# The last two attention batches' output projection taken from the attention loop into the token search's rounds, and their gate logits made from a product of weights

## The chip, the cores and the metric

The kernel runs on one core of one Trainium2 chip, as one program. The metric is the device time of one execution, in microseconds (us); the lower the better. The times given are of whole executions. "PE" is TensorE, "DVE" VectorE, "ACT" ScalarE, "POOL" GpSimd and "SP" SyncE, which here only issues DMAs.

## What is computed

The input is 16 batches of 256 tokens with 256 features. A first block (folding, style blend, a two-layer FFN) makes `x1`. Then comes attention with 16 heads of 64, and a layer of 8 experts, each of which takes the 512 tokens with the highest gate for it:

```
qkv = (h @ Wqkv.T).reshape(b, n, 3, H, HD)
...
attn = jax.nn.softmax(scores, axis=-1)
o = jnp.einsum('bhnm,bhmd->bhnd', attn, v)
o = o.transpose(0, 2, 1, 3).reshape(b, n, H * HD)
x = x + o @ Wout.T
tok = x.reshape(-1, d)
gate = jax.nn.softmax(tok @ Wgate.T, axis=-1)
vals, idx = jax.lax.top_k(gate.T, k_cap)
g = _ln(tok[idx_flat], mlp_g, mlp_b).reshape(k_cap, E, d)
...
tok = tok.at[idx_flat].add(y.reshape(-1, d))
```

The change turns on `x + o @ Wout.T` (called x2 in the kernel) and on `tok @ Wgate.T` (the logits). The logits of a batch can be had without its x2, as x1 Wgate' + o (Wout' Wgate').

## The kernel before

The program has four parts, each with its own instruction streams, and a barrier of all engines between them: the first block, attention, the token search, the experts. Every product whose inputs need full precision is made of three matmuls on a high and a low half of each input (`product`, L147; the halves' names end in `_h` and `_l`); a matmul on plain `ident`, `proj` or `wgate` is one float32 product, which shows as two rows in the trace.

**Attention** runs in steps t, and batch b = t has its scores and softmax in step t. A step has 8 pairs s of heads. For each pair PE does, in program order: 12 score matmuls (L1107), the 8 transposes of the pair before (L1119), perhaps a fill (a few transposes or small products into bank 0, `fill`), the next batches' qkv products (`chunk`), and the products with v (L1134). DVE takes the scores' minimum (L1493), ACT the exponentials (L1262), POOL multiplies by the reciprocal of the sum (L1392), ACT and DVE copy the transposed probabilities (`pT`). The scores of the next pair wait for the exponentials of this one, since both use the same two banks. The order is written out by hand in tables (`TR_FILLS`, `PROJ_PAIRS`, `values_at`).

The output projection of batch t-1 is two rows of tokens with 24 matmuls of 128x256 each, in pairs 2 and 3 of step t (`project`). x1 is loaded again and added, x2 is stored to `out`, its layer norm to `x2_rows`, and its transposes (`x2` fill, L1205, then copied to `proj`) and the product with `wgate` (`gates` fill, L1210) give the logits. The last step with scores is t = 15 ("closing"), and there are no `chunk`s left in it. In it batch 14's projection stands in pairs 2 and 3, and batch 15's own is made piece by piece behind its pairs (`project_last`, L1158). `finish` (t = 16) does what is left of batch 15: two pairs of values, the last pieces of its projection, x2, its norm and its logits.

**The token search** finds each expert's 512th largest gate, two bits at a time, in 15 rounds. In a round DVE counts with two tests (L1749) and ACT with one (Sign, L1660), PE adds the counts over partitions (L1677), and DVE picks the next trial value (L1760 to L1770). Between these PE runs `idle_products(6)` (L1591): products whose result nobody reads. Meanwhile SP loads weights of the first two experts (`split_*`, made in attention) and raw weights of the third. POOL has nothing to do. The experts then gather rows from `x2_rows` by indirect DMA.

## Time and profile before

| | |
|---|---|
| median of 3 executions | 1431.31 us (1430.86 to 1431.76) |
| profiled execution | 1430.09 us, of which the trace spans 1428.3 us |
| PE busy | 1370.0 us, 96% |
| ACT, DVE, POOL busy | 1035.7, 960.9, 912.5 us |
| scores of batch 0 begin | 364.0 us |
| pair 2 of step t = 15 begins | 1125.6 us |
| search begins (first DVE instruction) | 1166.2 us |
| experts begin | 1205.3 us |

A row of a timeline gives start and duration in us, engine, source line, operation, what is written and read, how often, and in square brackets how long the engine had been idle before it and for whom. A matmul row's end is modelled and lies behind the next row's start: rates are read from starts. `PEclk` is the granted share of the full TensorE clock of 2.4 GHz.

### The profile page before, as it was taken

What the parts mean: (1) busy time and instruction counts of PE and PEld (TensorE: products, weight loads), DVE (VectorE), ACT (ScalarE), POOL (GpSimd) and SP (SyncE); (2) the same over time, 40 slices, a digit from 0 to 9 for tenths busy, and PEclk for the clock granted to TensorE, in tenths of its full rate; (3) what the DMA queues carried; (4) which work ended last, traced back from release to release, by engine and by line L of the source; (5) the groups of instructions that cost most, each with busy time, mean ns of one, the idle gap of its engine ahead of it and who ended that gap; (6) DMA issues with size and microseconds to landing.
All of it is one profiled execution on the core that took longest, in us unless ns stands there. A gap on an engine that the chain in (4) does not pass through costs nothing. (4 is left out here: it accounts for less than half of the span.)

```text
span 1428.3 us, 30431 instructions
## 1 busy us (share of the span) xinstructions
PE 1370.0 (96%) x10795; PEld 1184.1 (83%) x10795; DVE 960.9 (67%) x2191; ACT 1035.7 (73%) x2703; POOL 912.5 (64%) x855
## 2 busy tenths in 40 slices
PE   7899999997999999999999999999999988999996
PEld 6799999996688887887888888788888678889896
DVE  6876677654776676676667667667756568678763
ACT  5566666565898889889889888988988732476662
POOL 2576666652678768867877876886777620354643
PEclk9899999999999999999999999999999999999999
DMA  5342222110100100110110010011011046145522
GB/s 159 122 122 67 68 68 69 50 51 23 38 9 31 53 23 31 53 45 9 53 46 31 31 53 28 26 53 45 9 45 46 31 143 258 45 104 155 138 34 30
DMA packets 61638, 89.04 MB, mean 62 GB/s; under 512 B 6144, under 2 KB 50992, under 8 KB 58800
## 3 DMA queue, kind: packets, MB, share of 16 engines
q1 hardware_dynamic: 53232, 75.82, 16.4%
q0 software_dynamic: 6144, 8.39, 3.6%
q10 hardware_dynamic: 2112, 2.88, 0.6%
q8 instruction: 87, 1.43, 0.4%
q14 instruction: 63, 0.52, 0.1%
HBM read 61.90 MB, written 25.18 MB: 61 GB/s over the span
## 5 line engine op out<-in xcount | busy, mean ns | idle before, releaser
L1392 POOL TENSOR_TENSOR prob<-prob,share_p 128x512 f32<-128x512 f32 x256 | 271.6, 1067 | 196.1 <-DVE share_p L1499 195.6
L1493 DVE TENSOR_REDUCE shift<-bank 128x2 f32<-128x512 f32 x256 | 164.7, 685 | 185.9 <-PE bank L1107 185.8
L1262 ACT ACTIVATE prob<-bank,shift 128x256 f32<-128x256 f32 x512 | 237.8, 479 | 63.9 <-DVE shift L1493 63.8
L147 PE MATMUL bank<-wqkv_h,rowsT_h 128*128 128x512 f32 x384 | 159.3, 415 | 2.0 <-PEq L311 1.7
L147 PE MATMUL bank<-wqkv_h,rowsT_l 128*128 128x512 f32 x384 | 151.7, 395 | 0.0
L147 PE MATMUL bank<-wqkv_l,rowsT_h 128*128 128x512 f32 x384 | 151.3, 394 | 0.0
L1119 PE MATMUL bank<-ident,prob 128*128 128x128 f32 x1024 | 143.0, 281 | 1.3 <-POOL prob L1392 1.3
L1380 POOL TENSOR_TENSOR landing<-landing,rq 128x512 f32<-128x512 f32 x128 | 131.1, 1046 | 10.1 <-DVE rq L1447 10.1
L1134 PE MATMUL bank<-pT,landing 128*64 128x256 f32 x1024 | 126.2, 386 | 1.7 <-ACT pT L1351 1.7
L1119 PEld LDWEIGHTS bank<-ident,prob 128*128 128x128 f32 x1024 | 109.6, 141 | 21.7 <-POOL prob L1392 4.2
L1262 ACT ACTIVATION_READ_ACCUMULATOR prob<-bank,shift 128x1 f32 x512 | 107.3, 210 | 0.0
L1286 ACT ACTIVATE landing<-bank,cols 128x512 f32<-128x512 f32 x128 | 101.9, 796 | 5.8 <-PE bank L1200 4.2
L644 POOL TENSOR_TENSOR hid_l<-hid,hid_h 128x512 fp32r<-128x512 f32 x64 | 86.3, 1358 | 30.6 <-ACT hid_h L540 29.9
L536 ACT ACTIVATE hid<-bank,cols 128x256 f32<-128x256 f32 x128 | 53.3, 470 | 68.1 <-PE bank L147 67.9
L1134 PEld LDWEIGHTS bank<-pT,landing 128*64 128x64 f32 x1024 | 67.3, 137 | 40.8 <-issue 9.2
L1107 PE MATMUL bank<-kT_h,qT_h 64*128 64x256 f32 x512 | 85.6, 330 | 3.1 <-ACT prob L1262 3.1
L1489 DVE TENSOR_REDUCE ssq<-raw_sq 128x8 f32<-128x512 f32 x128 | 85.8, 672 | 3.2 <-ACT raw_sq L1308 2.6
L1524 DVE COPY pT<-bank 128x512 f32<-128x512 f32 x128 | 87.1, 681 | 0.4 <-PE bank L1119 0.4
L1306 ACT ACTIVATE landing<-bank 128x512 f32<-128x512 f32 x128 | 80.0, 625 | 9.1 <-PE bank L147 9.0
L1200 PE MATMUL bank<-ident,landing 128*128 128x128 f32 x512 | 78.4, 276 | 8.2 <-ACT landing L1286 3.7
L147 PEld LDWEIGHTS bank<-wqkv_h,rowsT_h 128*128 128x128 f32 x384 | 73.2, 191 | 15.5 <-issue 2.4
L147 PEld LDWEIGHTS bank<-wqkv_h,rowsT_l 128*128 128x128 f32 x384 | 72.7, 189 | 15.7
(324 smaller groups left out, 4518.3 us busy)
## 6 DMA issues: line engine op xcount, KB each, us to landing
landing<-in_fc1s SPq DMA_DIRECT2D x6, 1024.0 KB, 4.9
landing<-in_fc2s SPq DMA_DIRECT2D x6, 1024.0 KB, 5.1
rows<-in_x SPq DMA_DIRECT2D x16, 256.0 KB, 2.9
xT<-in_xT SPq DMA_DIRECT2D x16, 256.0 KB, 2.7
x_again<-in_x SPq DMA_DIRECT2D x16, 256.0 KB, 2.8
x_rows<-x SPq DMA_DIRECT2D x16, 256.0 KB, 3.2
rows<-x_rows SPq DMA_DIRECT2D x16, 256.0 KB, 3.1
x<-x_rows SPq DMA_DIRECT2D x16, 256.0 KB, 2.9
```

The costliest lines, as they stand in the source:

```text
L147: last = nc.tensor.matmul(out, a, b, start=(n == 0), stop=(n == 3 * len(ks) - 1))
L644: nc.gpsimd.tensor_tensor(hid_l[:, 2 * g:2 * g + 2, :], hid[:, 2 * g:2 * g + 2, :], hid_h[:, 2 * g:2 * g + 2, :].bitcast(F32), ALU.subtrac ...
L1107: mm = nc.tensor.matmul(score_bank[side][:, n * T:(n + 1) * T], q[r, at, n * P:(n + 1) * P], k[r, at, :], start=(i == 0), stop=(i == 2))
L1119: last = nc.tensor.transpose(pT_bank[side][:, m * T + n * P:m * T + (n + 1) * P], prob[q % 2 * 2 + side][:, n, m * P:(m + 1) * P], ident[: ...
L1134: last = nc.tensor.matmul(values_bank(b, q)[side * HD:(side + 1) * HD, :], v[its][:, m, h * HD:(h + 1) * HD], pT[q % 2 * 2 + side][:, m, : ...
L1262: last = nc.scalar.activation(prob[at][:, n, :], score_bank[side][:, n * T:(n + 1) * T], ACT.Exp, bias=shift[:, at, n:n + 1], scale=-1.0, ...
L1286: nc.scalar.activation(raw_block(j), tr[:, :].rearrange("p (m n) -> p m n", m=4), ACT.Identity, bias=cols[:, g + 1:g + 2], scale=cols[:, g ...
L1380: nc.gpsimd.tensor_tensor(part, part, rq[:, n, c * 8:(c + 1) * 8].unsqueeze(2).to_broadcast([P, 8, HD]), ALU.mult).then_inc(normed, 1)
L1392: nc.gpsimd.tensor_tensor(prob[at][:, :, :], prob[at][:, :, :], share[:, at, :].unsqueeze(2).to_broadcast([P, TT, T]), ALU.mult).then_inc( ...
L1489: nc.vector.tensor_reduce(ssq[:, n, c * 8:(c + 1) * 8], raw_sq[c % 2][:, :].rearrange("p (h d) -> p h d", h=8), AX, ALU.add).then_inc(summ ...
L1493: nc.vector.tensor_reduce(shift[:, s % 2 * 2 + side, :], score_bank[side][:, :].rearrange("p (n m) -> p n m", n=TT), AX, ALU.min).then_inc ...
L1524: nc.vector.tensor_copy(pT[q % 2 * 2 + 1][:, :, :].rearrange("p m n -> p (m n)"), pT_bank[1][:, :]).then_inc(pT_dve, 1)
```

## The change

In words: `project_last` and the projections of batches 14 and 15 leave attention. `kept` holds the halves of the output projection's weights and of o in memory that outlives attention; batch 14's o is also stored to DRAM (`keep_o`, 8 DMAs of 256 KB) and read back in the search, while batch 15's stays in place. For the logits, batch 0's step makes `wc` = Wout' Wgate' on PE (`logit_weights`, after pair 0's chunks: 16 float32 products with 8 columns) from `woutT`, which SP loads into the four `pT` tiles; DVE splits it in pair 1. `logits_of` then multiplies `wc` (16 columns: high and low part of 8) with o, 16 matmuls a batch, and the `gates` fill adds two small products to bring them to the logits of x1, whose transposes now fill from the reloaded x1.

In the search PE does 32 `late_step`s of three 128x256 matmuls: four steps ahead of the rounds, three in each of rounds 0 and 1, two in each of rounds 2 to 12. Every eighth step (in rounds 1, 4, 8 and 12) also adds x1 by a product of `late_x` with `ident`. Fewer idle products stand behind them, so that one idle product goes for two matmuls; the six before the gates' transposes and the six behind them go too. ACT takes the rows out of the banks and does the layer norm within the rounds, with small steps on POOL. SP stores x2 and its norm at the end of the search. The second expert's first weights (2 MB) are loaded after the first gathers, since batch 14's o uses their tile. The raw piece of expert weights now lands in `ew_l`, so its next load waits for the store of the one before.

```
+LATE = 2
+LATE_FROM = NB - LATE
+O_STORED, LATE_STORED, WC_IN = 16 * 7, 32, 80
+LATE_ORDER = [NB - 1] + list(range(LATE_FROM, NB - 1))
...
+CLOSING_FILLS = {(NB - 1, 9): (NB - 2, "x2"), (NB - 1, 11): (NB - 2, "gates"), (NB - 1, 13): (NB - 1, "x2"), (NB, 3): (NB - 1, "gates")}
+LATE_PAIR = {False: PROJ_PAIRS[0], True: PROJ_PAIRS[1]}
...
+                def keep_o(b, qs):
+                    for q in qs:
+                        wait(sp, o_lo, PAIRS, b, q + 2)
+                        for n, part in enumerate((o_h, o_l)):
+                            sp.dma_start(o_kept[b - LATE_FROM][n][:, q * T:(q + 2) * T],
+                                         o_part(part, q, b % 2, 2).bitcast(F32)).then_inc(o_stored, 16)
+
                 def step(t, odd):
+                    if t == -1:
+                        for q in range(4):
+                            sp.dma_start(pT[q][:, :, :], a["woutT"][:, q * T:(q + 1) * T].rearrange("(k p) n -> p k n", p=P)).then_inc(wc_in, 16)
...
                         load_piece(0, 0)
+                    if is_late(t - 1) and live(t):
+                        keep_o(t - 1, (0, 2, 4, 6))
...
+                        sp.wait_ge(ew_stored, 32 * (t + 1))
                         load_piece(t + 1, 1 - odd)
...
+                def logit_weights():
+                    pe.wait_ge(wc_in, WC_IN + 64)
+                    for m in range(PAIRS):
+                        for k in range(KT):
+                            last = nc.tensor.matmul(o_bank[:, m * E:(m + 1) * E], pT[m // 2][:, k, m % 2 * P:(m % 2 + 1) * P], wgate[:, k, :],
+                                                    start=(k == 0), stop=(k == KT - 1))
+                    last.then_inc(wc_made, 1)
...
-                def project_last(k, its):
...
+                def logits_of(b, half, its):
+                    wait(pe, o_lo, PAIRS, b, 4 * half + 4)
+                    if half == 0:
+                        if live(b + 2):
+                            wait(pe, chunk_out, 12, b + 2, 7)
+                        else:
+                            wait(pe, chunk_out, 12, NB - 1, 12)
+                            wait(pe, out_proj, TT, b - 1, TT)
+                    for k in range(4 * half, 4 * half + 4):
+                        for n, part in enumerate((o_h, o_l)):
+                            last = nc.tensor.matmul(chunk_bank[0][0:2 * E, 0:T], wc[:, k, :], part[:, o_at(k, its), :],
+                                                    start=(k == 0 and n == 0), stop=(k == PAIRS - 1 and n == 1))
+                    if half == 1:
+                        last.then_inc(tr_proj, TT)
...
-                                last = nc.tensor.matmul(fill_bank(b)[:, n * E:(n + 1) * E], x2T[:, k, n * P:(n + 1) * P], wgate[:, k, :],
-                                                        start=(k == 0), stop=(k == KT - 1))
+                                last = nc.tensor.matmul(tr[:, n * E:(n + 1) * E], x2T[:, k, n * P:(n + 1) * P], wgate[:, k, :],
+                                                        start=(k == 0), stop=(k == KT - 1 and not is_late(b)))
+                            if is_late(b):
+                                last = nc.tensor.matmul(tr[:, n * E:(n + 1) * E], from_o[:, n * P:(n + 1) * P], parts_of[:, :], start=False, stop=True)
                         last.then_inc(tr_gates, 1)
...
                 def finish(t, its):
-                    fill(t, 1)
                     values(t - 1, PAIRS - 2, its)
                     transposes(t - 1, PAIRS - 1)
-                    project_last(PAIRS - 3, its)
+                    logits_of(t - 1, 0, its)
+                    values(t - 1, PAIRS - 1, its)
+                    logits_of(t - 1, 1, its)
                     fill(t, 3)
-                    values(t - 1, PAIRS - 1, its)
-                    project_last(PAIRS - 2, its)
-                    project_last(PAIRS - 1, its)
...
+                        if first(t) and s == 0:
+                            logit_weights()
+                        if first(t) and s == 2:
+                            pe.wait_ge(wc_done, NB + 2)
                         if not closing(t):
-                            if s in PROJ_PAIRS and live(t - 1):
+                            if s in PROJ_PAIRS and live(t - 1) and not is_late(t - 1):
                                 project(t - 1, PROJ_PAIRS.index(s), 1 - odd)
+                            if s == LATE_PAIR[False] and live(t - 1) and is_late(t - 1):
+                                logits_of(t - 1, 0, 1 - odd)
+                                logits_of(t - 1, 1, 1 - odd)
...
-                        if closing(t) and s in PROJ_PAIRS:
-                            project(t - 1, PROJ_PAIRS.index(s), 1 - odd)
-                        if closing(t) and s >= 4:
-                            for k in range(0 if s == 4 else s - 3, s - 2):
-                                project_last(k, odd)
                         if closing(t):
+                            if s == LATE_PAIR[True]:
+                                logits_of(t - 1, 0, 1 - odd)
+                                logits_of(t - 1, 1, 1 - odd)
...
+                def logits_out(b):
+                    wait(act, tr_proj, TT, b, TT)
+                    wait(act, tr_gates, 1, b - 1, 1)
+                    nc.scalar.activation(from_o[:, :], chunk_bank[0][0:2 * E, 0:T], ACT.Copy).then_inc(out_proj, TT)
...
+LATE_FIRST, LATE_STEPS = 4, [3] * 2 + [2] * 11 + [0] * 2
+TAKEN_IN, SPREAD_IN, NORMED_IN = {2: 0, 5: 1, 10: 2, 13: 3}, {3: 0, 7: 1, 11: 2, 14: 3}, {6: 0, 9: 1, 13: 2}
...
+                    load_late_x(0)
...
+                    for i in range(1, LATE):
+                        load_late_x(i)
+                        load_late_o(i)
+                    load_halves(sp, w1_in, (w1_h, w1_l), halves[0:2], 0)
                     for e in range(EARLY):
-                        load_halves(sp, w1_in, (w1_h, w1_l), halves[0:2], e)
                         load_halves(sp, w2_in, (w2_h, w2_l), halves[2:4], e)
+
                     load_raw(sp, w1_raw, a["fc1s"], EARLY, 0, 0)
                     load_raw(sp, w2_raw, a["fc2s"], EARLY, 0, 1)
                     sp.dma_start(b1[:, :], a["b1s"]).then_inc(b1_in, 16)
                     sp.dma_start(b2[:, :, :], a["b2s"].unsqueeze(0).to_broadcast([P, E, D])).then_inc(b2_in, 16)
+                    for i, b in enumerate(LATE_ORDER):
+                        sp.wait_ge(late_normed, NB + TT * (i + 1))
+                        for rows, tile, last in ((x2_rows, late_n[i], last_rows), (out, late_x[i], last_out)):
+                            sp.dma_start(rows[bass.ds(b * T, T), :].rearrange("(t p) d -> p t d", p=P),
+                                         tile[:, :, :]).then_inc(last if i == LATE - 1 else late_stored, 16)
+                    sp.wait_ge(late_stored, LATE_STORED + 32 * (LATE - 1))
...
+                    def take(i):
+                        act.wait_ge(late_made, NB + i + 1)
+                        nc.scalar.activation(row(late_x, i), late_bank(i), ACT.Copy, accum_out=late_sum[:, i:i + 1]).then_inc(late_taken, 1)
+
+                    def spread_of(i):
+                        act.wait_ge(late_taken, NB + i + 1)
+                        nc.scalar.activation(late_mean[:, i:i + 1], late_sum[:, i:i + 1], ACT.Copy, scale=-1.0 / D).then_inc(late_centred, 1)
+                        act.wait_ge(late_centred, NB + i + 1)
+                        nc.scalar.activation(late_dead[:, :], row(late_x, i), ACT.Square, bias=late_mean[:, i:i + 1],
+                                             accum_out=late_sq[:, i:i + 1]).then_inc(late_squared, 1)
+
+                    def norm(i):
+                        act.wait_ge(late_rooted, NB + i + 1)
+                        nc.scalar.activation(row(late_n, i), row(late_x, i), ACT.Identity, bias=late_shift[:, i:i + 1],
+                                             scale=late_root[:, i:i + 1]).then_inc(late_normed, 1)
...
+                        if n in TAKEN_IN:
+                            take(TAKEN_IN[n])
+                        if n in SPREAD_IN:
+                            spread_of(SPREAD_IN[n])
+                        if n in NORMED_IN:
+                            norm(NORMED_IN[n])
+                    norm(LATE * TT - 1)
...
-                    idle_products(6)
...
+                    def late_step(i, k):
+                        j, rows = i // TT, slice(i % TT * P, (i % TT + 1) * P)
+                        high, low = late_o[j]
+                        if k == 0 and i % TT == 0 and j > 0:
+                            pe.wait_ge(late_in[j], 16 + 48)
+                        if k == HW // P - 1 and i == 0:
+                            pe.wait_ge(late_in[0], 16 + 16)
+                        if k == 0 and i >= 2:
+                            pe.wait_ge(late_taken, NB + i - 1)
+                        for m, (o, w) in enumerate(((high, wo_h), (high, wo_l), (low, wo_h))):
+                            nc.tensor.matmul(late_bank(i), o[:, k, rows], w[:, k, :], start=(k == 0 and m == 0), stop=False)
+                        if k == HW // P - 1:
+                            nc.tensor.matmul(late_bank(i), ident[:, :], late_x[j][:, i % TT, :], start=False, stop=True).then_inc(late_made, 1)
+
+                    for k in range(LATE_FIRST):
+                        late_step(0, k)
+                    done = LATE_FIRST
...
-                        idle_products(6)
+                        for _ in range(LATE_STEPS[n]):
+                            late_step(done // (HW // P), done % (HW // P))
+                            done += 1
+                        idle_products(6 - LATE_STEPS[n] * 3 // 2, 2, 384)
...
+                    if t == -3:
+                        for half in gathered:
+                            sp.wait_ge(half, 32)
+                        load_halves(sp, w1_in, (w1_h, w1_l), halves[0:2], 1)
...
+                        if first(later):
+                            pool.wait_ge(last_rows, 16 * (LATE_FROM + 1))
```

PE in step t = 15's end and `finish`, before: the last rows ahead of the search. The six L1158 rows are the last piece of batch 15's projection.

```order
L1158 MATMUL bank<-wout_h,o_h 128x256
L1158 MATMUL bank<-wout_l,o_h 128x256
L1158 MATMUL bank<-wout_h,o_l 128x256
L1158 MATMUL bank<-wout_h,o_h 128x256
L1158 MATMUL bank<-wout_l,o_h 128x256
L1158 MATMUL bank<-wout_h,o_l 128x256
L1205 MATMUL bank<-ident,x 128x128 x4
L1210 MATMUL bank<-wgate,proj 128x8 x4
```

The same place in the changed kernel (L1157 transposes, L1172 values, L1194 `logits_of`, L1249 and L1252 the `gates` fill).

```order
L1157 MATMUL bank<-ident,prob 128x128 x8
L1194 MATMUL bank<-kept,wc 16x256 x8
L1172 MATMUL bank<-pT,landing 64x256 x4
L1194 MATMUL bank<-kept,wc 16x256 x8
L1249 MATMUL bank<-wgate,proj 128x8 x2
L1252 MATMUL bank<-parts_of,from_o 128x8
L1249 MATMUL bank<-wgate,proj 128x8 x2
L1252 MATMUL bank<-parts_of,from_o 128x8
```

The transposes of x stand two pairs earlier, and the projection's pieces between transposes and values are gone.

PE at the start of the search in the changed kernel, rounds 0 and 1; before, six L1591 products stood first, six behind the gates' transposes, and six in every round.

```order
L1813 MATMUL bank<-kept 128x256 x12
L1822 MATMUL bank<-ident,gates 128x128 x2
L1827 MATMUL bank<-base,same 128x4
L1830 MATMUL bank<-count,same 128x4
L1832 MATMUL bank<-base,same 128x4
L1813 MATMUL bank<-kept 128x256 x9
L1662 MATMUL bank<-ident 128x128 x2
L1830 MATMUL bank<-count,same 128x4
L1832 MATMUL bank<-base,same 128x4
L1813 MATMUL bank<-kept 128x256 x3
L1815 MATMUL bank<-late_x,ident 128x256
L1813 MATMUL bank<-kept 128x256 x6
```

The late matmuls stand between one round's total and the next one's, where the idle ones stood.

PE in step t = 0 of the changed kernel, from pair 0's last chunk to pair 1's scores (L1145, before L1107).

```order
L147 MATMUL bank<-wqkv_h,rowsT_h 128x512
L147 MATMUL bank<-wqkv_l,rowsT_h 128x512
L147 MATMUL bank<-wqkv_h,rowsT_l 128x512
L1130 MATMUL bank<-wgate,pT 128x8 x16
L1145 MATMUL bank<-kT_h,qT_h 128x256 x2
```

The L1130 row is new; before, the scores followed the chunk.

## Rows read from the trace of the kernel before

**Rows 1.** The page: busy time, and PE's granted clock in 40 slices.

```profile
PE 1370.0 (96%) x10795; PEld 1184.1 (83%) x10795; DVE 960.9 (67%) x2191; ACT 1035.7 (73%) x2703; POOL 912.5 (64%) x855
...
PEclk9899999999999999999999999999999999999999
```

**Rows 2.** Timeline of PE, t = 15: the first score row of pairs 2 to 7.

```profile
1125.58 0.38 PE L1107 MATMUL bank<-kT_h,qT_h 64*128 64x256 f32 x2
...
1131.60 0.39 PE L1107 MATMUL bank<-kT_h,qT_h 64*128 64x256 f32 x2
...
1137.60 0.38 PE L1107 MATMUL bank<-kT_h,qT_h 64*128 64x256 f32 x2
...
1142.17 0.39 PE L1107 MATMUL bank<-kT_h,qT_h 64*128 64x256 f32 x2
...
1146.01 0.39 PE L1107 MATMUL bank<-kT_h,qT_h 64*128 64x256 f32 x2
...
1149.85 0.39 PE L1107 MATMUL bank<-kT_h,qT_h 64*128 64x256 f32 x2
```

**Rows 3.** Timeline of PE, pair 2: first and last of 24 projection matmuls; pair 1's gates.

```profile
1124.60 1.06 PE L1210 MATMUL bank<-wgate,proj 128*128 128x8 f32 x8
...
1128.53 0.39 PE L147 MATMUL bank<-wout_h,o_h 128*128 128x256 f32 x1
...
1131.39 0.28 PE L147 MATMUL bank<-wout_h,o_l 128*128 128x256 f32 x1
```

**Rows 4.** Timeline, `finish` and the change to the search.

```profile
1156.32 0.69 DVE L1524 COPY pT<-bank 128x512 f32<-128x512 f32 x1 [0.17 <-PE bank L1119]
...
1158.08 1.08 PE L1134 MATMUL bank<-pT,landing 128*64 128x256 f32 x8
...
1159.62 0.42 DVE L1512 TENSOR_TENSOR o_l<-bank,o_h 128x256 fp32r<-128x256 f32 x1 [1.96 <-ACT o_h L1334]
...
1161.75 0.75 DVE L1517 TENSOR_TENSOR x<-bank,x 128x256 f32<-128x256 f32 x2 [1.70 <-DMA x<-x_rows]
...
1165.06 0.18 ACT L1293 ACTIVATE logit<-bank 128x16 f32<-128x16 f32 x1 [1.21 <-PE bank L1210]
...
1166.19 0.18 DVE L1704 MEMSET units<- 128x1 f32 x5 [0.87 <-PEq L1052]
```

**Rows 5.** Timeline, t = 0 (pairs 0 to 4): PE at the new products' place, and its waits.

```profile
367.86 0.39 PE L1107 MATMUL bank<-kT_h,qT_h 64*128 64x256 f32 x2
...
375.45 0.66 PE L1200 MATMUL bank<-ident,landing 128*128 128x128 f32 x4 [0.34 <-POOL landing L1380]
...
382.36 0.39 PE L1107 MATMUL bank<-kT_h,qT_h 64*128 64x256 f32 x2 [1.38 <-ACT prob L1262]
...
384.77 1.11 PE L1119 MATMUL bank<-ident,prob 128*128 128x128 f32 x4 [0.84 <-POOL prob L1392]
```

**Rows 6.** Timeline, a round of the search.

```profile
1176.52 0.51 ACT L1660 ACTIVATE signs<-key,trial 128x256 bf16<-128x256 f32 x1 [1.30 <-DVE trial L1770]
...
1177.33 0.08 DVE L1749 DVE_READ_ACCUMULATOR count_junk<-key,trial 128x1 fp32r x1
...
1177.47 0.27 PE L1677 MATMUL bank<-count,same 128*128 128x4 f32 x1
...
1177.71 1.58 PE L1591 MATMUL bank<-ident 128*128 128x128 f32 x12
```

**Rows 7.** Timeline of PE, first block: float32 products with 256 columns.

```profile
10.54 2.07 PE L388 MATMUL bank<-landing 16*128 16x256 f32 x4
```

**Rows 8.** Windows (stretch, length, each engine's busy time, PEclk, DMA share, GB/s).

```profile
380.00:384.00 4.00, 2.55 (x26) 1.97 (x23) 3.93 (x11) 3.60 (x11) 2.41 (x3) 1.00 0.00 0
384.00:387.00 3.00, 2.23 (x10) 2.14 (x11) 1.87 (x4) 1.25 (x5) 3.00 (x4) 0.53 0.78 252
1162.00:1166.00 4.00, 1.69 (x12) 1.39 (x12) 2.41 (x9) 0.78 (x2) 0.69 (x1) 0.98 0.19 66
1166.00:1169.00 3.00, 2.85 (x12) 2.63 (x12) 2.23 (x17) 0.42 (x1) 0.00 (x0) 0.50 0.70 184
```

232 lines of the change are left out of this document (138 added, 94 removed).

## The prediction

> **What bounds the kernel now.** I read the page first: PE is busy 96% of the span and its clock is granted nearly everywhere [rows 1]. So each added product costs its time wherever PE has no gap, and each removed one pays only where nothing else takes its place. The page can't say which of the two holds at the four places that the change touches; the timelines do.
>
> In step t = 15 the pairs take 6.02, 6.00, 4.57, 3.84 and 3.84 us (pairs 2 to 6, from the starts of their scores [rows 2]). The last two are the floor that no removal gets under: a pair's scores, DVE's minimum, four exponentials on ACT, and the next scores wait for them. The same floor shows in t = 0, where PE has nothing else to do and waits 1.38 us for ACT [rows 5]. Pairs 2 to 4 lie above it because of the projection.
>
> In the search a round takes 1.90 us, and it is DVE's chain that sets it: DVE's second count ends at 1177.41 and the total starts at 1177.47. The idle products are 12 rows from 1177.71 on that end 1.58 us later by a modelled end [rows 6]. I take 0.12 us a row, so they keep PE 12 x 0.12 = 1.44 us, and with the two small products ahead of them (0.24) PE needs 1.68 of the 1.90. Its slack is 0.22 us a round. ACT is idle 1.30 us before each Sign [rows 6].
>
> **The pairs of t = 15.** A projection of 128 tokens is 24 matmuls; their first and last starts are 2.86 us apart [rows 3], 0.12 us each, and the pair spends 3.07 us on them (1128.53 to 1131.60 [rows 2, 3]). Pair 2 loses one and falls to the floor: 6.02 to 3.85, -2.2. Pair 3 loses 24 and gets `logits_of(14)`, 16 matmuls that also stream 256 columns, 2.0 us: 6.00 to 4.95, -1.05; it stays above the floor. Pair 4 loses 12 (1.5 us) and gets four transposes: 4.57 to 3.85, -0.7. Pair 5 gets the `gates` fill. Before, pair 1's fill took 1124.60 to 1125.58 [rows 2, 3], 0.98 us for 8 rows; the two new products add 4 rows, 0.45. PE's work in a pair without extras is 2.95 us (1125.58 to 1128.53 [rows 2, 3]), so 2.95 + 0.98 + 0.45 = 4.4 against 3.84: +0.55. Pair 6 stays. Sum -3.4; I keep 0.6 either way, for the loss of the x2 work on DVE and POOL and for how well the copies of ACT fit in.
>
> **`finish` and the way to the search.** Pair 7's values can start once DVE's copy ends at 1157.01 [rows 4]; they started at 1158.08 because the gates of batch 14 and a piece of the projection stood ahead. Now only 8 matmuls (1.0 us) stand there, so about 1157.2: -0.87. The low half of o then ends at 1159.17 instead of 1160.04 [rows 4]. Before, from there: six matmuls, a wait for x1's DMA until 1161.75, two adds, transposes, copy, gates, logit at 1165.06 to 1165.24. Now: 8 matmuls (1.2 with the tail), ACT's copy of 16 rows (0.4), 12 gate rows (1.5), the logit (0.25): 1159.17 + 3.4 = 1162.6. The search's first DVE instruction came at 1166.19, 0.95 after the logit; batch 15's norm and its store are gone too, so I take 0.8: 1163.4. That is -2.8, between -2.2 and -3.2.
>
> **Step t = 0.** 16 float32 products are 32 rows. The nearest rows have the same weights' size and the same 8 columns: 8 in 0.98 us [rows 2, 3]. 32 cost 3.8 us, right before pair 1's scores, which started at 367.86 behind the chunk without a wait [rows 5]. Nothing covers it. What may give some back are the waits for POOL (0.34 and 0.84 [rows 5]) since POOL gets ahead while PE is held; the 1.38 is the floor and stays. Bounds +2.6 and +3.9; I put +3.8 in the sum and the return, 0.8, beside the clock below. The woutT load (1 MB at the start of attention) and DVE's split are over long before they are needed.
>
> The Trainium skill, "TensorE: Matmul & The Clock Gate", part 1, says that the distance of two matmuls' starts never drops below about 25 ns however small they are. By that floor 32 rows would cost 0.8 us and the sum below would be 3.0 lower. The row (0.12 us at 8 columns) disagrees by a factor of five here, as each of these products loads 128 new columns of weights; I go by the row.
>
> **The rounds.** Four steps ahead of the rounds run while PE would have idled. In the rounds three matmuls at 0.12 replace one and a half products of two rows: 6 matmuls + 6 rows is again 12. Round 0 has 13 units, within the slack. But rounds 1, 4, 8 and 12 add a float32 product of 256 columns. Four rows of 256 columns took 2.07 us at half clock [rows 7], so a product's two rows take 0.5 at full clock. Rounds 4, 8, 12: 0.24 + 1.44 + 0.5 + 0.1 for the change of kind = 2.28, +0.38 each; round 1: 2.5, +0.6. Sum +1.8, between 0 (if the matmuls pack tighter than the idle rows) and 3.3 (0.1 more in each of 15 rounds). ACT's new work in a round is one or two operations on 256 columns like Sign's 0.51 [rows 6], with a small one beside; it fits into the 1.30 idle, tightest in rounds 13 and 14, and POOL is free.
>
> **Loads and stores.** SP loads as much in the search as before but for 0.5 MB. The last rows' norm follows the last Sign by a square, three small POOL steps and itself; DVE still has the ranks to work out then, and the first gather needs indices that are only made in the experts' part. In attention the piece's later load waits for two stores, a pair or so, and is not read before pair 2 of the next step. All of this I put at 0; if that cover is gone, a late store holds the first gather, microsecond for microsecond.
>
> **Sum.** -3.4 - 2.8 + 3.8 + 1.8 = -0.6 us against the profiled execution's 1430.09.
>
> **The clock.** It is granted at 0.53 in 384 to 387 behind a stretch in which PE waited for ACT and POOL and was busy 2.55 of 4 us, and at 0.50 in 1166 to 1169 behind one with 1.69 of 4 us busy, among it 8 gate rows of 8 columns [rows 8]. A row pair that runs at 1.2 instead of 2.4 GHz takes double. The 3.8 us of narrow rows in t = 0 look more like the second of these stretches than like any full one, and dense chunks follow. If the clock falls there for as long as the 3 us of either low row, PE does half the work in them and loses about 1.7 with the edges. With the 0.8 that POOL's lead gives back I add 0.9: together +0.3. The median of the plain runs is 1.2 above the profiled one; I carry the difference over: 1431.3 + 0.3 = **1431.6 us**.
>
> **Rivals.**
> 1. *The terms nearly cancel* (as above), 1429 to 1434: chance 0.50.
> 2. *The clock falls and costs twice.* In t = 0 it is low during part of the narrow rows and during the chunks behind them (two low stretches, +3.4). At the search's start the six products behind the gates' transposes are gone, so PE stands still some 2 us right after a low stretch; if the clock is low in the first rounds, 13 rows take 3.1 us and a round costs 1.2 to 1.5 more. -0.6 + 3.4 + 1.5 = +4.3: 1435.6. It decides for slower from +2.9 on, which means a second low stretch. For it: rows 8. Against: most of the search's stretch is dense. Chance 0.25. The Trainium skill, same page, part 1, states that the throttled clock is the default and activity releases it; rows 8 agree with it in both places.
> 3. *The rows are cheap.* The narrow products cost near the page's floor, or PE's slack and POOL's lead swallow them, and the closing rounds fit: -0.6 - 3.0 = -3.6, 1427.7. For it: the idle rows' true need is not measured, only bounded. Against: 0.98 us for 8 narrow rows, 16 times in the trace. Chance 0.20.
> 4. *The last rows' store is late* and the first gather waits: each microsecond beyond its cover costs one, so 2 to 5 late gives 1433 to 1437. Against: by then nothing else is queued on SP. Chance 0.05.
>
> **Numbers.** About 0.2% (2.9 us) is what a measurement of this kernel can tell from no change. Faster by more: rival 3 and the low end of 1, 0.23. Slower: 2, 4 and the high end of 1, 0.27. Same: 0.50. Range: the lower bounds of the terms give -4.0 - 3.2 + 2.6 + 0.5 = -4.1, 1427.2; the upper end lies 0.9 above rival 2, for a round more at the low clock: 1436.5.
>
> **What would show each step.** In the changed profile: pairs 2 to 5 of t = 15 at 3.9, 4.95, 3.9, 4.4; the search's first MEMSET about 6.2 us less behind pair 2 than before; 32 narrow rows of 0.12 us in t = 0 and PEclk behind them; rounds 1, 4, 8, 12 at 2.3 to 2.5 and the others at 1.90; from the search's start to the experts 40.9 instead of 39.1. I'm wrong if other rounds grow too, if the narrow rows run at another rate, or if the first gather waits for the store.

## The result, and the profile after

The changed kernel takes 1435.06 us (median of 11 executions, 1429.36 to 1436.26), the kernel before 1431.32 us (11 executions on the same chip, 1428.83 to 1433.11). The ratio is 1.0024, with a 95% interval of 1.0015 to 1.0033: 3.7 us slower, more than the 0.2% that can be told from no change. The profiled execution of the changed kernel took 1433.18 us with a span of 1431.4, 3.1 more than the one before. Four executions among those of the experiments below took 1688 to 2651 us instead of about 1430; their ratios leave these out, their medians don't.

Taking the same points of both traces gives the balance (shift is after minus before, in us):

| point | before | after | shift | what this part added |
|---|---|---|---|---|
| scores of pair 1, t = 0 | 367.86 | 372.45 | +4.59 | +4.59 |
| scores of pair 2, t = 0 | 373.00 | 379.63 | +6.63 | +2.04 |
| scores of pair 0, t = 1 | 410.22 | 416.50 | +6.28 | -0.35 |
| scores of pair 2, t = 15 | 1125.58 | 1132.63 | +7.05 | +0.77 |
| scores of pair 7, t = 15 | 1149.85 | 1154.15 | +4.30 | -2.75 |
| first DVE instruction of the search | 1166.19 | 1168.22 | +2.03 | -2.27 |
| experts' first idle products | 1205.30 | 1209.77 | +4.47 | +2.44 |
| first fc1 of the experts | 1224.11 | 1227.39 | +3.28 | -1.19 |

PE's timeline of the changed kernel at t = 0, from pair 0's last chunk on. It answers to the score rows in [rows 5]:

```profile
364.02 0.39 PE L1145 MATMUL bank<-kT_h,qT_h 64*128 64x256 f32 x2
...
367.56 0.40 PE L147 MATMUL bank<-wqkv_h,rowsT_l 128*128 128x512 f32 x1
367.79 4.73 PE L1130 MATMUL bank<-wgate,pT 128*128 128x8 f32 x32
372.45 0.58 PE L1145 MATMUL bank<-kT_h,qT_h 64*128 64x256 f32 x2
...
374.03 1.97 PE L1157 MATMUL bank<-ident,prob 128*128 128x128 f32 x8
...
379.63 0.39 PE L1145 MATMUL bank<-kT_h,qT_h 64*128 64x256 f32 x2
...
388.66 0.39 PE L1145 MATMUL bank<-kT_h,qT_h 64*128 64x256 f32 x2 [1.37 <-ACT prob L1306]
391.07 1.11 PE L1157 MATMUL bank<-ident,prob 128*128 128x128 f32 x4 [0.85 <-POOL prob L1448]
```

The 32 narrow rows hold PE for 372.45 - 367.79 = 4.66 us. About 20 of them start before 370, 0.11 us each; the last 12 take 0.2 each. Pair 1 behind them takes 7.18 us (372.45 to 379.63) where it took 5.14, without a wait of its own: its eight transposes last 1.97 us, at full clock such a group lasts 1.09. Pair 2 takes 5.22 us instead of 5.55, since the wait of 0.34 for POOL [rows 5] is gone. The last two rows show that the waits for ACT and POOL further on are as long as before (1.37 and 0.85; 1.38 and 0.84 in [rows 5]), so POOL's lead gave back 0.3 and no more. The windows of the same stretch (PEclk, the granted clock, is the third number from the end):

```profile
core 0: us, PE busy (x) PEld busy (x) DVE busy (x) ACT busy (x) POOL busy (x), PEclk, DMA share, GB/s
364.00:370.00 6.00, 6.00 (x46) 5.34 (x45) 4.45 (x9) 5.87 (x18) 2.04 (x2) 1.00 0.00 0
370.00:374.00 4.00, 4.00 (x25) 3.78 (x24) 0.00 (x0) 0.02 (x1) 0.00 (x0) 0.51 0.00 0
374.00:377.00 3.00, 3.00 (x15) 2.95 (x14) 2.38 (x5) 1.13 (x5) 0.84 (x1) 0.51 0.00 0
377.00:380.00 3.00, 3.00 (x18) 2.25 (x18) 2.25 (x9) 3.00 (x9) 1.10 (x2) 1.00 0.35 93
```

PE counts as fully busy in all four, and yet it runs at 1.2 GHz from about 370 to 377. Neither PE's busy share nor that of its weight loads (PEld, 3.78 of 4 us from 370 on) tells such a stretch; the clock column does.

One trace could be chance, but there are four with these rows in t = 0 (the changed kernel, e4_search, e4_again and e9_behind below), and in each the clock is low from 370 or 371 to 377 or 378. In the ten others, that of the kernel before among them, it is 1.00 from 366 to 380.

PE's timeline from `finish` to round 1 of the search. It answers to [rows 4] and [rows 6]; L1194 are the logits' matmuls on wc, L1813 the late matmuls, L1815 a closer, L1662 the idle products:

```profile
1161.33 1.08 PE L1172 MATMUL bank<-pT,landing 128*64 128x256 f32 x8
1163.36 1.11 PE L1194 MATMUL bank<-kept,wc 128*16 128x256 f32 x8 [0.94 <-DVE kept L1575]
1165.02 0.64 PE L1249 MATMUL bank<-wgate,proj 128*128 128x8 f32 x4 [0.56 <-issue]
1165.59 0.59 PE L1252 MATMUL bank<-parts_of,from_o 16*128 16x8 f32 x2
1166.11 1.02 PE L1249 MATMUL bank<-wgate,proj 128*128 128x8 f32 x4
...
1168.19 2.90 PE L1813 MATMUL bank<-kept 128*128 128x256 f32 x12 [0.53 <-PEq L1064]
1171.27 0.69 PE L1822 MATMUL bank<-ident,gates 128*128 128x128 f32 x2 [0.18 <-DVE gates L1875]
1173.93 0.27 PE L1827 MATMUL bank<-base,same 128*128 128x4 f32 x1 [1.98 <-DVE same L1909]
...
1175.95 0.37 PE L1830 MATMUL bank<-count,same 128*128 128x4 f32 x1
1176.18 0.35 PE L1832 MATMUL bank<-base,same 128*128 128x4 f32 x1
1176.39 0.99 PE L1813 MATMUL bank<-kept 128*128 128x256 f32 x3
1177.18 1.05 PE L1815 MATMUL bank<-late_x,ident 128*128 128x256 f32 x2
1177.67 1.69 PE L1813 MATMUL bank<-kept 128*128 128x256 f32 x6
1179.20 0.61 PE L1662 MATMUL bank<-ident 128*128 128x128 f32 x4
1179.57 0.25 PE L1830 MATMUL bank<-count,same 128*128 128x4 f32 x1
```

PE stands still for 1.98 us where twelve idle rows stood, and round 1 takes 1179.57 - 1175.95 = 3.62 us instead of 1.90. Windows of the changed kernel over the same place:

```profile
1168.00:1172.00 4.00, 3.59 (x14) 2.92 (x14) 2.62 (x20) 0.42 (x1) 0.00 (x0) 0.50 0.47 142
1172.00:1176.00 4.00, 2.07 (x17) 2.07 (x17) 3.37 (x17) 1.20 (x4) 0.00 (x0) 0.93 1.00 349
1176.00:1179.00 3.00, 3.00 (x14) 2.82 (x14) 2.01 (x10) 1.08 (x4) 0.00 (x0) 0.50 1.00 421
```

Low, then nearly full while PE is busy 2.07 of 4 us, then low again during round 1. Rounds 4, 8 and 12 (each with a closer) take 2.05 to 2.07 us, rounds without one 1.88 to 1.93, but for round 6, which takes 2.42 as it did before. Round 4's closer and what stands behind it, at full clock:

```profile
1184.39 0.59 PE L1815 MATMUL bank<-late_x,ident 128*128 128x256 f32 x2
1184.82 0.83 PE L1662 MATMUL bank<-ident 128*128 128x128 f32 x6
1185.40 0.25 PE L1830 MATMUL bank<-count,same 128*128 128x4 f32 x1
```

### The profile page after: what moved, and what is told of

It is laid out like the page before. It is cut to its first block and busy times, and to the rows that moved or that the text cites. A ratio compares the mean times of both kernels' runs of the same rounds, so it can differ in the third digit from the quotient of the medians.

```text
span 1431.4 us, 30415 instructions
## 1 busy us (share of the span) xinstructions
PE 1370.6 (96%) x10769; PEld 1182.9 (83%) x10769; DVE 956.8 (67%) x2178; ACT 1042.8 (73%) x2727; POOL 912.8 (64%) x864
## 5 line engine op out<-in xcount | busy, mean ns | idle before, releaser
L147 PE MATMUL bank<-kept 128*128 128x256 f32 x1440 | 183.1, 285 | 0.0
L147 PEld LDWEIGHTS bank<-kept 128*128 128x128 f32 x1440 | 175.3, 191 | 0.0
L1157 PE MATMUL bank<-ident,prob 128*128 128x128 f32 x1024 | 144.5, 282 | 1.9 <-POOL prob L1448 1.9
L1157 PEld LDWEIGHTS bank<-ident,prob 128*128 128x128 f32 x1024 | 110.6, 142 | 23.1 <-POOL prob L1448 5.3
L1172 PE MATMUL bank<-pT,landing 128*64 128x256 f32 x1024 | 126.2, 386 | 3.1 <-ACT pT L1409 3.1
L656 POOL TENSOR_TENSOR kept<-hid,kept 128x512 fp32r<-128x512 f32 x64 | 86.3, 1357 | 31.0 <-ACT kept L552 30.4
L1172 PEld LDWEIGHTS bank<-pT,landing 128*64 128x64 f32 x1024 | 67.3, 136 | 42.8 <-issue 9.4
L147 PE MATMUL bank<-kept,w_h 128*128 128x256 f32 x512 | 95.8, 287 | 0.0
L147 PE MATMUL bank<-ew_h,kept 128*128 128x256 f32 x512 | 94.1, 282 | 0.0
L1145 PE MATMUL bank<-kT_h,qT_h 64*128 64x256 f32 x512 | 85.8, 331 | 4.0 <-ACT prob L1306 3.8
```

What stands on the lines that cost most here:

```text
L147: last = nc.tensor.matmul(out, a, b, start=(n == 0), stop=(n == 3 * len(ks) - 1))
L656: nc.gpsimd.tensor_tensor(hid_l[:, 2 * g:2 * g + 2, :], hid[:, 2 * g:2 * g + 2, :], hid_h[:, 2 * g:2 * g + 2, :].bitcast(F32), ALU.subtrac ...
L1145: mm = nc.tensor.matmul(score_bank[side][:, n * T:(n + 1) * T], q[r, at, n * P:(n + 1) * P], k[r, at, :], start=(i == 0), stop=(i == 2))
L1157: last = nc.tensor.transpose(pT_bank[side][:, m * T + n * P:m * T + (n + 1) * P], prob[q % 2 * 2 + side][:, n, m * P:(m + 1) * P], ident[: ...
L1172: last = nc.tensor.matmul(values_bank(b, q)[side * HD:(side + 1) * HD, :], v[its][:, m, h * HD:(h + 1) * HD], pT[q % 2 * 2 + side][:, m, : ...
```

## Experiments

Each was timed in five rounds beside the kernel before. Since the kernel before read 1431.32, 1431.98, 1430.72 and 1430.88 us in the four sets of runs, the ratios to it compare better than the medians. Experiments 1 to 4 ran in one set, 5 to 8 in the next, the last four in a third, each set on another chip.

| run | median us | ratio to before, 95% |
|---|---|---|
| changed kernel | 1435.06 | 1.0024 (1.0015 to 1.0033) |
| e1_dense | 1433.40 | 1.0009 (1.0001 to 1.0018) |
| e2_none | 1429.54 | 0.9985 (0.9976 to 0.9994) |
| e3_early | 1429.77 | 0.9988 (0.9979 to 0.9996) |
| e4_search | 1439.18 | 1.0051 (1.0038 to 1.0063) |
| e5_finish | 1429.94 | 0.9994 (0.9985 to 1.0003) |
| e6_open | 1428.18 | 0.9982 (0.9973 to 0.9991) |
| e7_both | 1428.95 | 0.9990 (0.9981 to 0.9999) |
| e8_close | 1427.50 | 0.9980 (0.9971 to 0.9989) |
| e9_behind | 1437.58 | 1.0047 (1.0034 to 1.0060) |
| e4_again | 1437.49 | 1.0048 (1.0035 to 1.0061) |
| e10_early_e4 | 1428.61 | 0.9987 (0.9977 to 0.9996) |
| e11_early_all | 1427.75 | 0.9978 (0.9970 to 0.9987) |

**e1_dense**: the narrow products against dense ones of as many rows.

```
-                    for m in range(PAIRS):
-                        for k in range(KT):
-                            last = nc.tensor.matmul(o_bank[:, m * E:(m + 1) * E], pT[m // 2][:, k, m % 2 * P:(m % 2 + 1) * P], wgate[:, k, :],
-                                                    start=(k == 0), stop=(k == KT - 1))
+                    last = nc.tensor.matmul(o_bank[:, 0:PAIRS * E], pT[0][:, 0, 0:P], wgate[:, :, :].rearrange("p k e -> p (k e)")[:, 0:1].to_broadcast([P, PAIRS * E]),
+                                            start=True, stop=True)
                     last.then_inc(wc_made, 1)
+                    for _ in range(15):
+                        nc.tensor.matmul(o_bank[:, 384:512], ident[:, :], ident[:, :], start=True, stop=True)
```

> Changed kernel with the 16 products of 8 columns in t = 0 (32 narrow rows) replaced by one product of 64 columns and 15 idle products of 128 x 128 on ident: as many float32 rows, but dense ones. The product of wout and the router's weights is left out, so wc holds other numbers. Theory A (the narrow rows let the clock fall, and the pair behind them pays double): the rows still cost about 3.9 us, but pair 1 behind them takes 5.1 us again instead of 7.2, PEclk stays at 1.00 from 368 to 380; 1432.7, that is 2.4 below the changed kernel. Theory B (only the time of the rows counts, and the clock falls in t = 0 for another reason, or its fall only moves): a low stretch stays within 368 to 380 and the time stays within 0.5 of the changed kernel's, 1435.

It came out 0.15% (2.1 us) below the changed kernel, theory A's side; each of the two ratios is good to 0.09%, so the time alone would be thin. The trace decides it. Its timeline and windows at t = 0:

```profile
366.07 0.39 PE L1145 MATMUL bank<-kT_h,qT_h 64*128 64x256 f32 x2
...
369.83 0.33 PE L1128 MATMUL bank<-wgate,pT 128*128 128x64 f32 x2
370.00 3.57 PE L1132 MATMUL bank<-ident 128*128 128x128 f32 x30
373.50 0.39 PE L1145 MATMUL bank<-kT_h,qT_h 64*128 64x256 f32 x2
...
378.64 0.39 PE L1145 MATMUL bank<-kT_h,qT_h 64*128 64x256 f32 x2
```

```profile
370.00:374.00 4.00, 4.00 (x40) 3.88 (x41) 1.15 (x2) 2.04 (x6) 1.15 (x2) 1.00 0.00 0
374.00:377.00 3.00, 3.00 (x27) 2.64 (x25) 2.01 (x5) 1.77 (x6) 0.47 (x1) 1.00 0.00 1
377.00:380.00 3.00, 3.00 (x24) 2.30 (x23) 2.93 (x11) 3.00 (x10) 1.87 (x3) 1.00 0.28 87
```

30 rows of 128 columns and two of 64 take 3.67 us, and pair 1 behind them 5.14, all at 1.00. So the rows with sixteen times the columns came out cheaper: at full clock a row costs about the same (0.12 and 0.11 us), and behind these the clock stayed. The dense rows differ from the narrow ones in more than width: they read one tile, `ident`, which is mostly zeros, again and again. The experiment shows that it isn't the number of rows; width and contents it doesn't tell apart.

**e2_none** takes the narrow products out, but for one.

```
-                    for m in range(PAIRS):
-                        for k in range(KT):
...
+                    last = nc.tensor.matmul(o_bank[:, 0:PAIRS * E], pT[0][:, 0, 0:P], wgate[:, :, :].rearrange("p k e -> p (k e)")[:, 0:1].to_broadcast([P, PAIRS * E]),
+                                            start=True, stop=True)
```

> Changed kernel with the 16 products of 8 columns in t = 0 replaced by a single one of 64 columns: the product of wout and the router's weights is left out, so wc holds other numbers. Theory A (rows 3.8 to 4.6, and their low clock 2): t = 0 costs nothing more than before, 6.3 below the changed kernel, 1428.8, below the kernel before by 2.5. Theory B (what t = 0 lost comes back by itself as later waits shrink or grow): 3.8 or less is won, 1431.3 or more.

0.39% (5.6 us) below the changed kernel: theory A. With e1_dense this splits the price of t = 0: 0.24% (3.5 us) for the rows' time, 0.15% (2.1 us) for what they do to the clock. The traces give 3.4 and 3.0, by the way from pair 0's scores to pair 2's (15.61 us in the changed kernel, 12.57 in e1_dense, 9.17 in e2_none). That the whole gained less has a place in the traces too: rounds 0 and 1 of the search both run at the low clock in e1_dense and e2_none (6.99 and 6.97 us together), while the changed kernel's trace has 5.64.

**e3_early** puts them into gaps of step t = -1.

```
+WEIGHTS_AT = {5: (0, 1), 7: (1, 4), 8: (4, 6), 10: (6, 7), 12: (7, 8)}
-                        if first(t) and s == 0:
-                            logit_weights()
+                        if t == -1:
+                            logit_weights(2 * s)
                         fill(t, 2 * s)
...
+                            if t == -1:
+                                logit_weights(2 * s + 1)
                             fill(t, 2 * s + 1)
```

> Changed kernel with the same 16 products of 8 columns spread over half-pairs 5, 7, 8, 10 and 12 of step t = -1, ahead of idle fills in which PE waits 0.6 to 2.0 us each for something else; nothing is left out. Theory A (these gaps are free): all of the 6.3 us of t = 0 goes, or 5.5 if two of the gaps are too short; 1429. Theory B (the gaps are there since PE is ahead of a chain that its fills belong to, so that a product put in them pushes the chain, or the clock falls there instead): half of it or more stays, 1431 to 1433.

0.36% (5.2 us) below the changed kernel and 0.12% below the kernel before: theory A. The scores of pairs 0 to 3 of t = 0 start at 364.01, 367.87, 372.99 and 378.55, within 0.01 us of the kernel before: the gaps were free. Not all that its trace gains over the kernel before is the change's doing: step t = 0 takes 44.82 us against 46.21, since the low stretch of 384 to 387 [rows 8] isn't there. But its search opens worse than the changed kernel's:

```profile
1155.00:1158.00 3.00, 1.76 (x14) 1.34 (x14) 0.42 (x1) 0.54 (x2) 0.00 (x0) 1.00 0.00 0
1158.00:1162.00 4.00, 3.47 (x18) 3.36 (x19) 1.53 (x15) 0.60 (x2) 0.00 (x0) 0.57 0.22 49
1162.00:1166.00 4.00, 1.84 (x8) 1.14 (x7) 2.92 (x14) 0.60 (x2) 0.00 (x0) 0.50 0.82 257
1166.00:1170.00 4.00, 4.00 (x20) 4.00 (x20) 2.27 (x12) 0.60 (x2) 0.00 (x0) 0.50 1.01 420
1170.00:1172.00 2.00, 2.00 (x9) 1.82 (x9) 1.28 (x7) 1.07 (x4) 0.00 (x0) 0.50 0.97 406
```

One unbroken low stretch from the finish on; rounds 0 and 1 take 3.44 and 3.60 us.

**e4_search** changes the search and leaves t = 0 as it is.

```
                     last.then_inc(tr_gates, 1)
+                    idle_products(6, 2, 384)
                     for n in range(DIGITS):
...
-                        idle_products(6 - LATE_STEPS[n] * 3 // 2, 2, 384)
+                        idle_products(6 - LATE_STEPS[n] * 3 // 2 - (2 if n in (1, 4, 8, 12) else 0), 2, 384)
```

> Changed kernel with six idle products back behind the gates' transposes at the search's start, and two idle products fewer in each of rounds 1, 4, 8 and 12, where a closing product of 256 columns is added; nothing is left out. Theory A (the stand-still of PE at the start makes the second low stretch, and round 1 takes 3.6 us for it): round 1 is 1.9 again, rounds 4, 8 and 12 1.9 instead of 2.05; 2.1 below the changed kernel, 1433.0. Theory B (the clock falls there anyway, owing to the way that the finish goes): only the closing rounds give back, 0.45; 1434.6, with a low stretch still between 1172 and 1180.

Neither theory: 0.27% (3.9 us) above the changed kernel. In its profiled execution (1434.33 us, the fastest of six) the rounds are as meant, 1.90 in rounds 1, 4, 8 and 12. The other five took 1437.05 to 1439.88 with a mean granted clock of 0.977 to 0.982 against 0.983 in the profiled one. By the mean clock, that is more time at 1.2 GHz; no trace shows where.

**e5_finish, e6_open, e7_both** fill gaps of e3_early with idle products: e5_finish by the `idle` lines in `finish` (and a wait for ACT's last exponentials ahead of them, since they write to a scores' bank), e6_open by the two `idle_products(6, 2, 384)`, e7_both by all.

```
                 def finish(t, its):
+                    wait(pe, exped, H, t - 1, H)
+                    idle(4)
                     values(t - 1, PAIRS - 2, its)
...
+                    idle(3)
                     logits_of(t - 1, 1, its)
+                    idle(2)
                     fill(t, 3)
...
                     done = LATE_FIRST
+                    idle_products(6, 2, 384)
                     pe.wait_ge(gated, 1)
...
                     last.then_inc(tr_gates, 1)
+                    idle_products(6, 2, 384)
```

> The kernel with the early narrow products (e3_early, 1429.8) with nine idle products more in the finish, in gaps in which PE waits: four ahead of the values of pair 6 (a gap of 1.13 us), three ahead of the second half of the logits (0.94), two ahead of the gates (0.56); nothing is left out. Theory A (it is PE's standing still in the finish that starts the 13.7 us low stretch from 1158 on): the stretch is gone or shorter, rounds 0 and 1 take 1.9 us each again instead of 3.4 and 3.6; 1426.7, 3.1 below e3_early. Theory B (the stand-still behind the finish, at the search's start, does it): the low stretch only starts later and still covers both rounds; 1429.5 to 1430.5.

> e3_early with twelve idle products more at the search's start: six behind the four late steps, where PE waits for the gates, and six behind the gates' transposes, where it waits for the first counts (1.98 us); nothing is left out. Theory A (those two gaps keep the low stretch going once it has begun): it ends earlier, round 1 at least is 1.9 again; 1428.0, 1.8 below e3_early. Theory B (at half clock the idle products take 2.9 us for six and push the gates' transposes and the first base product): 1431 to 1434. The run in which six of these products and fewer in the closing rounds gave 1439.2 speaks for B.

> e3_early with the idle products of both e5_finish and e6_open; nothing is left out. If the finish alone starts the low stretch, the twelve at the start are free at full clock: 1426.7 as e5_finish. If only both gaps together keep the clock: 1426.5, with e5_finish and e6_open at 1429 or above. If the clock falls whatever PE does there: 1431 to 1434.

e5_finish is not below e3_early (0.9994 against 0.9988; the intervals overlap). Its windows:

```profile
1160.00:1165.00 5.00, 4.35 (x34) 3.96 (x32) 1.21 (x14) 0.73 (x3) 0.00 (x0) 1.00 0.07 8
1165.00:1168.00 3.00, 0.62 (x4) 0.20 (x2) 2.20 (x9) 0.32 (x2) 0.00 (x0) 1.00 0.64 195
1168.00:1172.00 4.00, 2.99 (x14) 2.99 (x15) 2.88 (x15) 1.13 (x4) 0.00 (x0) 0.57 1.03 389
```

The finish and the late steps now run at full clock, but in the next stretch PE is busy 0.62 of 3 us and the clock falls behind it, over rounds 0 and 1 as before (3.44 and 3.53). That is theory B: a low stretch comes later and the time stays. e6_open and e7_both brought rounds 0 and 1 back to 2.01 and 2.19, and 2.01 and 2.18. e6_open's ratio is 0.06% below e3_early's, not the 0.12% of theory A, and the intervals overlap. The price named in its theory B is also paid: from pair 7's scores to the first base product it takes 1168.54 - 1147.42 = 21.1 us instead of 1165.67 - 1146.48 = 19.2, since twelve idle rows at half clock stand ahead of the gates' transposes. Idle products in the finish added nothing to that: e7_both's 0.9990 is no better than e3_early's 0.9988, and none of the three times expected of it (1426.5, 1426.7, 1431 or more) came.

**e8_close** is e3_early with the second edit of e4_search.

> e3_early with two idle products fewer in each of rounds 1, 4, 8 and 12, nothing else; nothing is left out. It undoes one half of what e4_search did. Theory A (rounds 4, 8 and 12 are 0.15 longer for PE's work alone): 0.45 to 0.6 below e3_early, 1429.2. Theory B (this half cost e4_search its 4 us, by low stretches within the search): 1433, with a low stretch behind one of these rounds.

0.9980: theory B's 1433 is out. Rounds 4, 8 and 12 take 1.90 again, as theory A has it, and round 1 3.14 instead of 3.60; together 0.9 us in the trace, and 0.08% (1.1 us) was measured, with intervals that overlap e3_early's. e4_search's loss isn't this half's.

**e9_behind, e4_again, e10_early_e4, e11_early_all** follow that loss and look for the best version. e9_behind is the first edit of e4_search alone, e10_early_e4 both edits on e3_early, e11_early_all the edits of e6_open and e8_close together.

> The changed kernel with one half of e4_search alone: the six idle products behind the gates' transposes; nothing is left out. Theory A (e4_search's 1439.2 belongs to these products): 1438 or more. Theory B (it belongs to the pair of edits, or to that set of runs and not to the code): 1433.5, 1.5 below the changed kernel, from round 1 at 1.9 instead of 3.6.

> e4_search once more, unchanged, beside e9_behind on one chip. If its 4 us over the changed kernel are the code's, 1438 to 1440 again, and its low stretches in the slower runs tell where; if they were that set's, 1433, as its profile alone would have it (1434.3 with rounds 1, 4, 8 and 12 at 1.90).

> e4_search's two edits on e3_early, where nothing is left of the narrow products in t = 0; nothing is left out. From the traces so far: the way from pair 7 to the first base product and rounds 0 and 1 take 23.9 in e4_search, 26.2 in e3_early, 25.9 in e8_close; rounds 4, 8 and 12 give 0.45. Theory A (the pieces add): 1427.0, 2.7 below e3_early. Theory B (e4_search's edits cost wherever they stand): 1433 or more.

> e6_open (1428.2) and e8_close (1427.5) together: e3_early with twelve idle products at the search's start and two fewer in each closing round; nothing is left out. If the two gains add (e6_open's 0.06% and e8_close's 0.08% below e3_early): 1427.0. If fewer idle products in round 1 undo what the twelve hold (round 1 was 2.18 in e6_open): round 1 at half clock and 1428 or more.

e4_again repeats e4_search, and e9_behind gives the same loss by the six products behind the gates' transposes alone: 1.0047, 0.23% above the changed kernel. On e3_early the same six cost less (e10_early_e4 0.9987 against e8_close's 0.9980, intervals overlapping); e10_early_e4 is no faster than e3_early (0.9988), so the pieces didn't add, and it is far from theory B's 1433. In e9_behind's trace the clock stays at 0.50 through them (from 1169 to 1179), where the changed kernel's had 0.93 from 1172 to 1176, and rounds 0 and 1 take 3.43 and 3.05:

```profile
1171.35 2.76 PE L1662 MATMUL bank<-ident 128*128 128x128 f32 x12
1174.01 0.37 PE L1828 MATMUL bank<-base,same 128*128 128x4 f32 x1
```

e11_early_all is the fastest version by its ratio, 0.9978, with e8_close (0.9980) no different within the intervals. Round 1 stays at 1.90 with two idle products fewer, so the second outcome named ahead is out. Its timeline shows the search's start as it was meant:

```profile
1161.88 2.90 PE L1819 MATMUL bank<-kept 128*128 128x256 f32 x12 [0.53 <-PEq L1065]
1164.58 2.56 PE L1668 MATMUL bank<-ident 128*128 128x128 f32 x12
1166.98 0.38 PE L1829 MATMUL bank<-ident,gates 128*128 128x128 f32 x2
1167.19 1.50 PE L1668 MATMUL bank<-ident 128*128 128x128 f32 x12
1169.34 0.27 PE L1835 MATMUL bank<-base,same 128*128 128x4 f32 x1 [0.64 <-DVE same L1917]
...
1171.36 0.27 PE L1838 MATMUL bank<-count,same 128*128 128x4 f32 x1
...
1173.26 0.27 PE L1838 MATMUL bank<-count,same 128*128 128x4 f32 x1
```

Rounds 0 and 1 take 2.02 and 1.90. It is 0.22% below the kernel before (3.1 us) and 0.46% (6.6 us) below the changed one, with nothing left out.

## Why the prediction came out as it did

The forecast was 1431.6 and "same"; 1435.06 came. It lies inside the range, but by the prediction's own line of 2.9 us it is slower, which was given 0.27 against 0.50, and it is closest to rival 2 (1435.6), which was given 0.25. The step that failed is the clock: "PE does half the work in them and loses about 1.7 with the edges. With the 0.8 that POOL's lead gives back I add 0.9". The narrow rows and pair 1 lost 3.2 us at the low clock instead of 1.7, POOL gave back 0.3, and a second low stretch stood over round 1.

How close rival 2's number came is partly luck. It had 7.2 us for t = 0, which took 6.3; the pairs and `finish` gave 1.2 less than the sum; and two shifts of +0.77 and -1.19 stood in no term.

- **Step t = 0** was put at +3.8 for the rows and is +6.3. Their own time is 32 x 0.11 = 3.5 us by the rows at full clock (and 3.5 for as many dense ones, e2_none against e1_dense), so the price by the nearest row was nearly right, and the floor of rival 3 is out. The rest is the clock: the trace has it low from about 370 to 377, not for 3 us, over the last 12 narrow rows and most of pair 1. Of POOL's 0.8, 0.33 came back.
- **The pairs of t = 15** gave -2.75 against -3.4. Pairs 2 and 4 fell to 3.72, a little under the floor of 3.85, and pair 6 did too. The prediction read the 3.84 of pairs 5 and 6 as the wait for ACT, but PE had no wait in them, it was full with six matmuls of the projection; with a wait for ACT (0.70, in pair 2) a pair takes 3.72. Pair 3 took 5.64 instead of 4.95, 0.51 of it in a wait for POOL's probabilities that the sum hadn't; pair 5 took 4.72 instead of 4.4.
- **`finish`** gave -2.27 against -2.8, within its range. The last values started right behind DVE's copy, as said (its end at 1161.19, they at 1161.33); the gates' rows then ran mostly at the low clock (1.02 us for four rows, 0.61 in step 15).
- **The rounds** took +2.44 against +1.8, but in other places: rounds 4, 8 and 12 cost 0.15 to 0.17 each instead of 0.38, and round 1 cost 1.7 instead of 0.6, at the low clock. That is rival 2's second half. In round 4 the closer takes 0.43 us (1184.39 to 1184.82), not 0.5 and 0.1 for the change of kind, and the six idle rows 0.58 (to 1185.40), not 0.72. The 0.5 was worked out from [rows 7] as rows at half clock; the profile grants 1.00 from 10.5 to 12 us, so no row bore it out. In the range's low end stands +0.5, where the low end of this term is 0.
- **Not foreseen**: +0.77 in steps 1 to 14, about 0.05 a step and spread over the pairs, which e3_early has as well (+0.78 from t = 1 to pair 2 of t = 15). Which instruction costs it wasn't tried. There is also -1.19 in the experts' start, where the low stretch was shorter (the clock is 0.51 from 1220 to 1223.5; before it was 0.63 from 1216 to 1220 and 0.51 from 1220 to 1224).
- **Loads and stores** were put at 0, rightly. SP waits 1.5 us for a store of x2 at the search's end, off the path: from the last count to the experts' first idle products it takes 6.41 us (1203.36 to 1209.77), before 6.40.

Between the rivals the choice was wrong where it leant on "most of the search's stretch is dense" and on one low stretch of 3 us as the measure of all. In [rows 8] stood a warning: rows of 8 columns, with idle time around them, stood there when the clock fell at 1166, and t = 0 has four times as many. It was no proof, as the other low stretch, at 384, has none. The Trainium skill, "TensorE: Matmul & The Clock Gate", part 1, states that activity releases the clock and that the throttled one is the default. The traces agree as far as the clock is not always granted, and comes back while PE goes on working (at 377, in the middle of pair 1). But e1_dense and the changed kernel show PE equally busy from 370 to 374 (4.00 of 4 us), and are granted 1.00 with the dense rows and 0.51 with the narrow ones, so the profile's busy share could not have been used to apply it. The same part's floor of about 25 ns between two matmuls' starts did not bind here: the narrow rows took 0.11 us each. That is no disagreement, as the prediction had it, since a floor says only that they can't be faster.

What stays open: why six idle products behind the gates' transposes cost 3.3 us in the changed kernel. The mean clock points to low stretches. The ratios of e4_search, e4_again and e9_behind count 16 executions. Five had a mean clock of 0.983 or 0.984, and four of these took 1434.07 to 1435.73 us, like the changed kernel's own at that clock (1433.18 to 1435.84); the fifth took 1437.05. The eleven at 0.977 to 0.982 took 1437.05 to 1439.88. The one trace of each run, its fastest execution, doesn't show where. Open too is whether the narrow rows' width or their contents let the clock fall.

## What to carry to other kernels

Price narrow float32 products twice: once by their rows (here 0.11 to 0.12 us each, at 8 columns as at 128), and once by the clock of what stands behind them. Look for gaps that already exist, ahead of a fill that waits for another engine: put there, these products cost nothing that the trace shows. Work that fills an engine's idle time must leave the round's own chain its slack: three closing rounds lost 0.15 us each until two idle products were taken out. Idle products put in to hold the clock should be timed, not assumed: here they brought it back for the first rounds in three versions (e6_open, e7_both, e11_early_all) and not in e9_behind, and while it is low twelve of their rows take 2.8 us instead of 1.5, ahead of whatever waits behind them.

## What the runs showed of the hardware

- The spread of one kernel's executions follows its mean granted clock. The kernel before, in the three sets of runs of the experiments, took a median of 1430.3 us in the 44 executions with a mean clock of 0.987 or more, and 1432.0 in the 41 below; the two at 0.991 took 1428.3 and 1428.5, the one at 0.982 took 1434.3.
- Some low stretches are fixtures and some are draws. The clock is at 0.50 from 346 to 348 us in all 14 traces, and low from 371 to 377 in all four with narrow rows in t = 0. The stretch of 384 to 387 [rows 8] is not there in e3_early, whose PE is busy 3.23 of 4 us from 384 to 388 as the kernel before is. And e4_search and e4_again, the same program, have round 0 at 2.87 and 2.01 us.
- Rows of 8 columns cost about as much of PE's time as rows of 128 (0.11 us each at full clock in the changed kernel; 32 dense ones in 3.67 us in e1_dense), but not the same of its clock: 0.51 from 370 to 377, against 1.00.
